# A four-layer mixed kernel: one activation table set for a softplus, the first row of maxima from another queue, loads and tokens issued at other points

## The reference, cut to what matters

```python
xn = _layernorm(x, axis=-1)
x = x + _L0_attn_ref(xn, ...) + _L0_ffn_ref(xn, ...)   # selective scan (Mamba) | routed experts, top 2
xn = _layernorm(x, axis=-1)
x = x + _L1_attn_ref(xn, ...) + _L1_ffn_ref(xn, ...)   # causal attention, 16 heads | routed experts, top 2
xn = _layernorm(x, axis=-1)
x = x + _L2_attn_ref(xn, ...) + _L2_ffn_ref(xn, ...)   # attention | dense runs of tokens through 8 experts
xn = _layernorm(x, axis=-1)
x = x + _L3_attn_ref(xn, ...) + _L3_ffn_ref(xn, ...)   # gated attention unit | routed experts, top 1
```

## Time and profile before

| | |
|---|---|
| median of three runs | 1991.06 us |
| profiled execution | 1985.47 us |
| its span | 1983.8 us |
| busy in the span: PE, DVE, ACT, POOL | 1555.5, 1341.1, 1044.5, 798.3 us |
| mean granted TensorE clock | 0.905 of full speed |
| transfers | 130.35 MB, mean 66 GB/s |

### The profile page before, as it was taken

How to read it: one execution, slowest core, us unless ns; L and a number is a source line. 1 busy time by engine, 2 the same in 40 slices (tenths; PEclk the granted TensorE clock), 3 DMA queues, 4 the chain that set the end, 5 groups by cost and what they waited for, 6 DMA issues and landing times. The chain is left out here.

```text
span 1983.8 us, 35609 instructions
## 1 busy us (share of the span) xinstructions
PE 1555.5 (78%) x12142; PEld 1065.2 (54%) x12143; DVE 1341.1 (68%) x2371; ACT 1044.5 (53%) x1857; POOL 798.3 (40%) x803
## 2 busy tenths in 40 slices
PE   5985887888865666636788889995489999869995
PEld 5753665665643444514566666663134444357884
DVE  7537777788799999585533337885873499556336
ACT  1458787787754545143433335663465477633441
POOL 1576555555698887257111113443320000006006
PEclk9997999999988888567899999997689999959998
DMA  4311111111000100456411113530652144021223
GB/s 146 99 62 52 52 38 46 51 34 46 17 26 25 31 23 10 161 186 159 70 44 44 42 44 68 89 62 20 175 88 51 33 67 66 5 90 54 87 79 85
DMA packets 153319, 130.35 MB, mean 66 GB/s; under 512 B 18929, under 2 KB 137864, under 8 KB 152914
## 3 DMA queue, kind: packets, MB, share of 16 engines
q1 hardware_dynamic: 140626, 104.57, 21.2%
q0 software_dynamic: 12544, 23.82, 4.6%
HBM read 77.08 MB, written 52.43 MB: 65 GB/s over the span
## 5 line engine op out<-in xcount | busy, mean ns | idle before, releaser
L667 POOL TENSOR_TENSOR xn_t<-xn_t,scan_du 128x512 f32<-128x512 f32 x256 | 321.6, 1270 | 179.9 <-ACT xn_t L809 100.0
L712 PE MATMUL banks<-scan_hc,ident 128*128 128x256 f32 x1024 | 294.9, 414 | 76.7 <-DVE scan_hc L864 76.7
L858 DVE TENSOR_TENSOR_SCAN xn_t<-banks,xn_t 128x512 f32<-128x512 f32 x256 | 311.3, 1216 | 42.0 <-ACT banks L799 35.7
L2287 ACT ACTIVATE att_pr<-banks 128x768 f32<-128x768 f32 (+1 forms) x256 | 234.2, 916 | 135.0 <-PE banks L2179 77.9
L799 ACT ACTIVATE banks<-delta,scan_exp_centre,a_neg 128x255 f32<-128x255 f32 x512 | 265.2, 559 | 49.9 <-DVE xn_t L858 49.4
L712 PEld LDWEIGHTS banks<-scan_hc,ident 128*128 128x128 f32 x1024 | 192.8, 207 | 139.6 <-DVE scan_hc L864 105.1
L864 DVE TENSOR_TENSOR scan_hc<-xn_t,banks 128x512 f32<-128x512 f32 x256 | 175.9, 687 | 26.8 <-PE banks L697 15.1
L918 POOL DMA_INDIRECT disp<-xn_tok,places x128 | 136.1, 1063 | 85.5 <-issue 61.3
L2332 DVE TENSOR_REDUCE att_mb<-banks 128x4 f32<-128x1024 f32 x128 | 153.9, 1221 | 22.9 <-PE banks L2146 18.1
L2195 PE MATMUL banks<-att_pr,att_vx 128*32 128x256 f32 (+1 forms) x2048 | 153.0, 372 | 5.0 <-ACT att_ot L2292 3.5
L2328 DVE TENSOR_REDUCE att_mb<-banks 128x6 f32<-128x768 f32 x128 | 121.5, 956 | 39.0 <-PE banks L2153 37.0
(11 more groups left out here) (360 smaller groups left out, 3340.0 us busy)
## 6 DMA issues: line engine op xcount, KB each, us to landing
scan_ew<-f_packed SPq DMA_DIRECT2D x12, 578.0 KB, 4.1
q_parts<-att_p_parts SPq DMA_DIRECT2D x16, 384.0 KB, 3.9
k_parts<-att_p_parts SPq DMA_DIRECT2D x16, 384.0 KB, 5.9
att_qs<-q_parts SPq DMA_DIRECT2D x64, 96.0 KB
att_ks<-k_parts SPq DMA_DIRECT2D x64, 96.0 KB
gau_ew<-f_packed SPq DMA_DIRECT2D x8, 578.0 KB
disp<-zeros SPq DMA_DIRECT2D x1, 4608.0 KB, 15.9
att_xin<-disp SPq DMA_DIRECT2D x72, 64.0 KB, 1.8
```

The costliest lines, as they stand in the source:

```text
L667: nc.gpsimd.tensor_tensor(bu[:, i % RING], b_sb[:, q % 2], du[:, b % 2, c:c + 1, :].to_broadcast([P, 2, T]), ALU.mult).then_inc(s.bu_made, 1)
L712: ins = nc.tensor.matmul(bank(Y_BANK)[:, c, :], g.ident[:], hc[:, i % RING, n, :], start=False, stop=(i % (PAIRS * DC) == PAIRS * DC - 1 a ...
L858: v.tensor_tensor_scan(rows(h[:, i % 2]), g.ps[:, DA + i % RING, :], rows(bu[:, i % RING]), 0.0, ALU.mult, ALU.add).then_inc(s.scan_done, 1)
L2287: nc.scalar.activation(pr[:, i % RING], g.ps[:, at:at + 2, 0:W], ACT.Exp, scale=scale).then_inc(s.p_ready, 1)
```

## The change

It has five parts.

1. **Front, split of B/C.** The middle part now goes to rows 0 to 63 of `bc3` in one copy. Rows 64 to 95 keep the high part, and the low part is written to rows 32 to 63. `lower` has one copy of 64 partitions instead of two of 32.
2. **Front, softplus.** ACT loads one table set that holds Exp and Ln. The logarithm of a chunk follows the exponential of the next one, DVE's addition (`finish`) stands between its other work, and the loads of the tables of Ln and of Exp at the end are gone.
3. **Scatter.** POOL no longer waits for its last indirect transfer. Who reads the table still waits for it.
4. **Start of both attentions.** ACT issues `top(0)` itself behind its copy, and then waits until all chunks are stored. SP waits only for the chunk that a load reads.
5. **First tokens of layer 1.** SP issues the loads of tiles 0 and 1 in the third batch, after `load(6)`. The loads of the others stay where they were.

```diff
 def lower(ch):
     act.wait_ge(s.rem_done, ch + 1)
-    nc.scalar.copy(bc3[W:2 * W, cols(ch)], rem[W:2 * W, ch % 2])
-    nc.scalar.copy(bc3[2 * W:3 * W, cols(ch)], rem[2 * W:3 * W, ch % 2]).then_inc(s.copied, 1)
+    nc.scalar.copy(bc3[0:2 * W, cols(ch)], rem[0:2 * W, ch % 2]).then_inc(s.copied, 1)
...
+def logarithm(ch):
+    act.wait_ge(s.exp_done, ch + 1)
+    nc.scalar.activation(e[:, :, cols(ch)], e[:, :, cols(ch)], ACT.Ln, bias=1.0).then_inc(s.ln_done, 1)
...
-nc.scalar.preload_act_table(ACT.Exp)
+nc.scalar.preload_act_table_set("natural_log_exp_and_others")
...
-for ch in range(BESIDE, NCH):
+for ch in range(3, NCH):
     exponent(ch)
+    logarithm(ch - 1)
+    if ch == BESIDE:
+        absolute(BESIDE + 2)
 act.wait_ge(f.scan_in, 48)
 nc.scalar.activation(f.a_neg[:], f.a_neg[:], ACT.Exp).then_inc(s.neg_a, 1)
-act.wait_ge(s.exp_done, NCH)
-nc.scalar.preload_act_table(ACT.Ln)
-for ch in range(NCH):
-    nc.scalar.activation(e[:, :, cols(ch)], e[:, :, cols(ch)], ACT.Ln, bias=1.0).then_inc(s.ln_done, 1)
-nc.scalar.preload_act_table(ACT.Exp)
+logarithm(NCH - 1)
...
 take(BESIDE + 2)                        # DVE
+finish(0)
+finish(1)
 give(BESIDE + 2)
+for ch in range(2, NCH - 1):
+    finish(ch)
 ...
+finish(NCH - 1)
...
 def scatter(...):
-    pool.wait_ge(done, 16 * (tiles[-1] + 1) * top)
...
 job.first_tokens                        # grouped()
+def first_tokens(sp):
+    sp.wait_ge(r.scattered, 2 * NT * 16)
+    for j in range(2):
+        sp.dma_start(xin[:, j, :], disp[j * P:(j + 1) * P, :]).then_inc(x_in[j], 16)
 def sync(sp):
-    sp.wait_ge(r.scattered, 2 * NT * 16)
-    def body(j, it, p, before, after):
+    def body(j, p):
         sp.wait_ge(s.turned, j + 1)
         sp.dma_start(xin[:, p, :], disp[bass.ds(j * P, P), :]).then_inc(x_in[p], 16)
-    each(sp, body)
+    with sp.Fori(1, NJ // 2) as it:
+        for p in range(2):
+            body(it * 2 + p, p)
...
-for p in range(PB):                     # end of projections' sync
-    sp.wait_ge(stored[p], len(range(p, NCH, PB)) * 32)
+def chunk_stored(eng, ch):
+    eng.wait_ge(stored[ch % PB], (ch // PB + 1) * 32)
+def all_stored(eng):
+    for ch in range(NCH - PB, NCH):
+        chunk_stored(eng, ch)
...
 def load(b):                            # SP, attention
+    if b % 2 == 0:
+        parts.chunk_stored(sp, b // 2)
     for half in range(2):
         load_half(sp, b, half)
 parts.sync(sp)
 load(2)
-top(0)
 for b in range(BATCH - 1):
-    top(b + 1)
+    top(sp, b + 1)
...
+    if moe and (b + 2) * PAIRS == MID:
+        job.first_tokens(sp)
...
 nc.scalar.copy(mt[:, (b + 1) % 2, :], ...).then_inc(s.mt_ready, 1)   # ACT
+if b == -1:
+    top(act, 0)
+    parts.all_stored(act)
```

More of the change, by code:

```diff
@@ L451, in _ @@
                 lower(BESIDE + 1)
+                logarithm(0)
                 absolute(BESIDE)
+                high(BESIDE + 2)
                 exponent(2)
-                high(BESIDE + 2)
+                logarithm(1)
+                lower(BESIDE + 2)
                 absolute(BESIDE + 1)
-                exponent(3)
-                lower(BESIDE + 2)
-                exponent(4)
-                absolute(BESIDE + 2)
-                for ch in range(BESIDE, NCH):
+                for ch in range(3, NCH):
                     exponent(ch)
+                    logarithm(ch - 1)
+                    if ch == BESIDE:
+                        absolute(BESIDE + 2)
                 act.wait_ge(f.scan_in, 48)
                 nc.scalar.activation(f.a_neg[:], f.a_neg[:], ACT.Exp).then_inc(s.neg_a, 1)
-                act.wait_ge(s.exp_done, NCH)
-                nc.scalar.preload_act_table(ACT.Ln)
-                for ch in range(NCH):
-                    nc.scalar.activation(e[:, :, cols(ch)], e[:, :, cols(ch)], ACT.Ln, bias=1.0).then_inc(s.ln_done, 1)
-                nc.scalar.preload_act_table(ACT.Exp)
+                logarithm(NCH - 1)
             @block.vector
@@ L489, in give, with finish @@
                     dve.wait_ge(s.copied, ch + 1)
-                    low = bc3[2 * W:3 * W, cols(ch)]
-                    nc.vector.tensor_tensor(low, rem[2 * W:3 * W, ch % 2], low, ALU.subtract).then_inc(s.split_done, 1)
+                    low = bc3[W:2 * W, cols(ch)]
+                    nc.vector.tensor_tensor(low, rem[W:2 * W, ch % 2], low, ALU.subtract).then_inc(s.split_done, 1)
+                def finish(ch):
+                    dve.wait_ge(s.ln_done, ch + 1)
+                    d = delta[:, :, cols(ch)]
+                    nc.vector.scalar_tensor_tensor(out=d, in0=d, scalar=0.0, in1=e[:, :, cols(ch)],
+                                                   op0=ALU.max, op1=ALU.add).then_inc(s.delta_done, 1)
                 job.vector(dve)
@@ L507, in _ @@
                 take(BESIDE + 2)
+                finish(0)
+                finish(1)
                 give(BESIDE + 2)
+                for ch in range(2, NCH - 1):
+                    finish(ch)
                 dve.wait_ge(s.neg_a, 1)
                 nc.vector.tensor_scalar(f.a_neg[:], f.a_neg[:], -1.0, None, ALU.mult).then_inc(s.neg_a, 1)
-                for ch in range(NCH):
-                    dve.wait_ge(s.ln_done, ch + 1)
-                    d = delta[:, :, cols(ch)]
-                    nc.vector.scalar_tensor_tensor(out=d, in0=d, scalar=0.0, in1=e[:, :, cols(ch)],
-                                                   op0=ALU.max, op1=ALU.add).then_inc(s.delta_done, 1)
+                finish(NCH - 1)
 def state_selection(nc, pool, sel, filled):
@@ L909, in _, with scatter @@
                 add(BATCH - 1)
-def scatter(nc, pool, done, src, disp, r, top, tiles=range(NT), pace=lambda i: None):
+def scatter(nc, pool, done, src, disp, r, top, tiles=range(NT)):
     for i in tiles:
-        pace(i)
         for k in range(top):
@@ L2076, in attention, with top @@
         steps = range(-LEAD, NP + PAIRS)
+        def top(eng, b):
+            eng.wait_ge(s.mt_ready, b + 1)
+            for half in range(2):
+                eng.dma_start(qs[half * HR + KR:half * HR + KM, b % BUFS],
+                              mt[half * 2 * PAIRS:(half + 1) * 2 * PAIRS, b % 2, :]).then_inc(mx_in[b % 2], 16)
         with nc.Block() as block:
@@ L2082, in load @@
                 def load(b):
+                    if b % 2 == 0:
+                        parts.chunk_stored(sp, b // 2)
                     for half in range(2):
                         load_half(sp, b, half)
-                def top(b):
-                    sp.wait_ge(s.mt_ready, b + 1)
-                    for half in range(2):
-                        sp.dma_start(qs[half * HR + KR:half * HR + KM, b % BUFS],
-                                     mt[half * 2 * PAIRS:(half + 1) * 2 * PAIRS, b % 2, :]
-                                     ).then_inc(mx_in[b % 2], 16)
                 parts.sync(sp)
                 load(2)
-                top(0)
                 for b in range(BATCH - 1):
-                    top(b + 1)
+                    top(sp, b + 1)
                     if b == 0:
```

2 lines of the change are left out of this document (added).

## The result

The changed kernel takes **1975.14 us** (median of four runs, 1966.74 to 1979.66), the kernel before 1990.92 beside it (1989.99 to 1992.78). The ratio is 0.9921, 95% interval 0.9899 to 0.9944: 15.8 us faster, 11 to 20 with the interval. A second series gave 0.9924 (0.9897 to 0.9951). Forecast were 23.8 us and a time of 1967.3. The time lies 7.8 above it: inside the whole range (1960 to 1976), which takes in the rivals, but above the forecast's own (1962 to 1973).

The account below looks back on a forecast made before the run. The prediction took waits at particular places to bound the kernel, with no engine busy over 78%. Gains of 5.6, 7.8, 4.3 and 6.1 summed to 23.8 us, so 1967.3 us; own range 1962 to 1973, whole range 1960 to 1976.

Parts of the forecast that it names:

- Slower: Rival: in the scan, Exp from the new table set takes longer; 1995 us or more, chance 0.03.
- given back at step 12: Rival: in layer 1's attention the scatter holds `load(3)`, so the 7.8 us are lost; 1975.1 us, chance 0.04.
- The front, 5.6 forecast: Front of layer 0: DVE ends at 156.8 and the scan starts at 157.7; 5.6 us gained, bounds 4.0 and 6.5.
- (a) to (d): Front: three copies fewer 1.9, Ln table load gone 1.28, ACT's wait filled 1.85, DVE's end 1.4; sum 6.5 us.
- even 5 us of landing stay inside 156.8: Front: POOL's last transfer, issued at 151.0, lands before DVE ends, so removing its wait counts as nothing.
- term (c): Front: ACT's wait of 1.85 us for `delta` gets filled with logarithms.
- The row of maxima, 7.8 and 6.1 forecast: Attention starts, layers 1 and 2: ACT issues the row at once, scores 4.9 us later; gains 7.8 and 6.1 us.
- held up behind `load(2)`: Rival: at both attention starts PE sees the row only once `load(2)` has landed; gains 5.9 and 3.8, 1971.5 us, chance 0.16.
- signs of being wrong: ACT's first exponential waits for the stores, scores wait until `load(2)` has landed, or a later stall grows by what was won.
- The tokens, 4.3 forecast: Experts of layer 1: tile 2 turned 5.4 us earlier, less a loss to PE's cold clock; 4.3 us, bounds 3.2 and 5.4.

Follow-up runs that it names:

- e1: Kernel before with only the front's changes (one copy, one table set, POOL's wait gone); 1986.17 us, ratio 0.9996.
- e5: Kernel after with the front's scatter leaving out the last four token tiles, and the scan's wait to match; one run, 1969.45 us.
- e4: Kernel before with only the loads of tiles 0 and 1 moved into the third batch in layer 1; 1983.53 us, ratio 0.9983.
- e6: Kernel after, but in both attentions SP issues the first row of maxima, ahead of `load(2)`; 1969.09 us, ratio 0.9892.
- e2: Kernel before with only the front's changes, but POOL keeps its wait for its last scatter transfer; 1989.49 us, ratio 1.0006.
- e3: Kernel before with only the start of both attentions changed (ACT issues the row, SP's loads wait by chunk); 1981.30 us, ratio 0.9963.
- e8: Kernel after, unchanged, run again beside the kernel before; 1973.69 us, ratio 0.9924.
- e9: Kernel after, but DVE holds the additions of chunks 2 to 6 until POOL has issued all its transfers; 1967.99 us, ratio 0.9917.
- e7: Kernel after, but in layer 1 SP issues the loads of token tiles 2 and on ahead of `load(7)`; 1970.91 us, ratio 0.9908.
- e10: Kernel after, with tiles 2 and on loaded ahead of `load(7)` in layer 1, and SP issuing the row ahead of `load(2)` in layer 2; ratio 0.9902.
- e12: Kernel after; layer 1: tiles 2 and on ahead of `load(7)`, half of `load(2)` ahead of SP's row; layer 2: row ahead of `load(2)`; ratio 0.9898.

## Why the prediction was right, and where not

**Direction and order of size: right.** All five parts do what was laid out, none is seen to cost time, and the loss of a rival's kind (`Slower`, the new set's Exp) isn't there: the scan's exponentials take 559 ns each in the kernel after too, as in the earlier trace rows. The measured 1975.1 is also the number of the rival *given back at step 12*; that is a coincidence. From the copy to the end of that wait it is 30.4 us on average over seven profiles with ACT's issue and 35.2 over four without, so 4.7 of the 5.2 us won in layer 1 are kept there.

**The front, 5.6 forecast: the step on POOL failed.** The terms (a) to (d) were right or low: DVE ended 7.3 us earlier, of which 0.7 was there at the table load already (131.19 and 130.46), so 6.6. What failed is "even 5 us of landing stay inside 156.8. I cost it at nothing". Two things were wrong in it. The issue end of 151.0 was taken from a front in which DVE's eight additions came behind the scatter; the change lays them beside it, and POOL ended at 154.75. And the price between POOL's last transfer and the next section is 6.17 us (7.50 with the wait), where 5 was only a supposition: before, the row showed 12.34 us there, which DVE covered. Even from 151.0 it would have given 157.1, nearly the forecast. So 5.6 became 2.4 in the pair of profiles, and 0.8 by e1's ratio. e5 shows that the 5 us between DVE's end and the start of the scan are POOL's.

Part of the spread of that term is PE's clock. In the kernel before, the four matmuls that feed ACT's wait of 1.85 us took 3.78 us at a granted clock of 0.50; in e4, whose front is the same code, they took 1.98 at 1.00, the wait was absent, and the scan started at 160.67:

```profile
140.72 1.98 PE L372 MATMUL banks<-front_dtx,front_w_dt 128*128 128x512 f32 x4 [3.19 <-DVE front_dtx L478]
```

So term (c) is there in some executions only. The mean start of the scan over the three profiles with the old front is 162.2, over the seven with the whole change 161.4. That is 0.8 us, as e1's ratio has it, so of the pair's 2.4 a good part is luck in which executions were profiled.

The Trainium skill states what may lie beneath POOL's slowing (SBUF — State Buffer, Who interferes with whom): a DVE instruction with two SBUF inputs contends with a GpSimd instruction that reads SBUF, and the order of issue decides who blocks. The additions have two such inputs, and the trace agrees: 3.00 us beside 2.35 us of them in every profile with the new front, and 1.96 against 0.97 us by 0.13 us in who starts first. The same section tells of a `tensor_tensor` that didn't stall a transfer; here the subtraction of B/C, which is one, did (1.33 us), and the measurement decides. I hadn't weighed it, and it spoke against this edit.

**The row of maxima, 7.8 and 6.1 forecast: the duration from issue to scores failed.** I took 4.9 us from rows in which SP issued the row behind its load and gave 3.4 and 6.4 as bounds; it is 7.45 and 7.73. The gains were 5.2 and 3.3 (below the bounds), and 5.2 and 3.8 on average over the profiles with and without ACT's issue. That is the rival "held up behind `load(2)`", which had 5.9 and 3.8, at a chance of 0.16, and one of the prediction's own signs of being wrong (the scores wait until `load(2)` has landed). e6 settles it: 3.1 us with nothing of the load ahead. What misled me is that the old 4.9 and 3.4 already had a load ahead, but one whose issue had begun 5 us before, when the stores had landed. Part of it was still to come: the engines' share was 0.95 from 910 to 912 us and 0.63 from 912 to 914. With the earlier issue the load went out on top of the stores; the transfer engines were as full as in the earlier trace rows:

```profile
895.00:900.00 5.00, 3.65 (x44) 2.77 (x46) 3.37 (x7) 0.36 (x1) 3.78 (x5) 0.50 0.98 321
```

The last two numbers are their share, 0.98, and GB/s. The stores alone don't hold the row: in e6 it had them ahead too, and in layer 2 of the kernel after the last store landed at 1416.45, 6.3 us ahead of the scores. The rule of the Trainium skill that an increment lands only after every earlier write of its engine, across queues (DMA: Bandwidth & Descriptors, Queues, rings and completion order), agrees with the 7.45 us of the kernel after beside the 3.1 of e6; taking turns between queues, which the same section states, did not let the row pass. Whether it was the data or the increment that waited, no run here shows.

**The tokens, 4.3 forecast: right within what can be told.** From first scores to the last turned tile the profiled pair gained 2.1 us; over the profiles with SP's old order (before, e1, e2, e3) it is 279.0 on average, over those with the new one (after, e4, e8, e9) 275.1, so 3.9; e4's ratio gives 3.4. The wait for tile 2 came as said (4.33). The cold clock came too (0.50), and fell on tiles 2 and 3.

**The sum.** 2.4 + 5.2 + 3.3 + 2.1 = 13.0 in the pair; the median gained 15.8 and the pair 18.7. The 5.7 between lie in stretches that the change doesn't touch, in an execution whose clock was 0.007 higher; by the line through all runs that is worth 5.5. The median fell 8 us short of the forecast, the terms of the pair 10.8: 3.2 in the front, 5.4 in the row, 2.2 in the tokens. The whole range held because it took in the row's rival; the forecast's own range did not.

**Still open.** What the 6.17 us behind POOL's last transfer consist of; and whether e7's order has a price ahead of tile 0, which comes 63.0 to 66.8 us behind the copy in the four profiles with it and 64.5 to 66.3 in five without. The 3.8 us between POOL's ends (150.98 and 154.75) are accounted for: the two early additions make 2.0, three later ones 1.7 and a subtraction 0.4, and POOL came to that stretch 0.3 sooner.

## What to carry to other kernels

When an edit makes the engine ahead of a barrier faster, find the next one by its own time to the barrier, not by the end of its last instruction, and ask whether the work that is moved now lies beside that engine and slows it. A small urgent transfer costs what is issued ahead of it: here 3 us without a load ahead and 7.5 behind one, on another engine's queue too; put it first where the load has slack, and leave it where the load has none. Take a duration for a moved transfer only from a row with the same backlog.

## What the hardware showed

- An indirect transfer issued by POOL takes 0.97 us of its engine; beside two DVE additions of two 128x1024 f32 operands it takes 3.00, beside later ones 0.97 to 2.01. What decides is whether the DVE instruction had started first: begun 0.10 us before the transfer it made it 1.96, begun 0.03 us behind it 0.97. The long ones of the front end 0.84 or 0.85 us behind the end of the DVE instruction. The same is in the kernel before, in layer 1, where one beside an addition of 4.42 us takes 4.77.
- A section that ends in such a transfer opens the next 6.17 us behind it, in eight profiles, with no wait in the program; 7.50 with one.
- The row's two transfers of 8 KB were seen 2.8 to 3.1 us behind their issue with nothing of the load ahead and the last stores still landing (e6, e10, e12), and after 7.45 and 7.73 with six and nine transfers of the load ahead as well.
- A table load in the front took 1.28 us with at most 0.02 us of gap on either side, and with one set for Exp and Ln the scan's Exp still took 559 ns.
